# A graph-network step on one core: a dense half in loops of four groups with its input loaded twice, and index copies one group ahead of the indirect transfers

## The reference

```python
h = relu(layernorm(x)); x = x + L0(h)   # three mean-aggregating dense layers
h = relu(layernorm(x)); x = x + L1(h)   # mean of (h[src]-e) by dst and of (h[dst]-e) by src, three products, batch norm
h = relu(layernorm(x)); x = x + L2(h)   # message sum by dst, then a GRU cell on every node
h = relu(layernorm(x)); x = x + L3(h)   # mean by src of h[dst] @ W.T + b
```

## Time and profile before

| | us |
|---|---|
| median of 3 runs | 7257.24 |
| lowest and highest | 7256.88 and 7260.77 |
| the profiled execution | 7259.3 |
| its span | 7257.6 |
| PE busy in the span | 4886.5 (67%) |
| DVE busy | 3986.4 (55%) |
| ACT busy | 2906.5 (40%) |
| POOL busy | 4063.4 (56%) |

### The profile page before, as it was taken

One profiled execution on the slowest core, in us unless ns is written; L12 is line 12 of the kernel. 1 busy time (PEld: TensorE's weight loads), 2 busy tenths in 40 slices (PEclk: granted clock), 3 DMA queues, 4 the chain that ended last, 5 costly groups with the idle time before them and its releaser, 6 DMA issues. The chain is left out here.

```text
span 7257.6 us, 107414 instructions
## 1 busy us (share of the span) xinstructions
PE 4886.5 (67%) x23937; PEld 3569.4 (49%) x23937; DVE 3986.4 (55%) x14866; ACT 2906.5 (40%) x6394; POOL 4063.4 (56%) x4659
## 2 busy tenths in 40 slices
PE   4776735558687687733655636699999978844553
PEld 2454524335565466633553324476666644434553
DVE  5665646654564455743323205566999989843210
ACT  0565634433463364323101100246888855533000
POOL 0655556630550353666565660475888877655556
PEclk9998867779899898865788877557999989955766
DMA  2233346659458655954546537443444444434443
GB/s 84 95 109 101 108 148 192 193 170 326 142 179 273 199 175 186 293 161 135 157 145 140 103 43 227 139 129 133 172 170 171 170 138 146 122 105 123 79 70 47
DMA packets 1124775, 1088.58 MB, mean 150 GB/s; under 512 B 106450, under 2 KB 986241, under 8 KB 1124197
## 3 DMA queue, kind: packets, MB, share of 16 engines
q1 hardware_dynamic: 983746, 911.02, 39.7%
q0 software_dynamic: 140800, 175.08, 11.3%
HBM read 651.65 MB, written 456.06 MB: 153 GB/s over the span
## 5 line engine op out<-in xcount | busy, mean ns | idle before, releaser
L1058 POOL DMA_INDIRECT G_x<-node_table,G_idx x400 | 398.5, 996 | 165.6 <-issue 130.0
L1058 POOL DMA_INDIRECT G_V<-layer_rows,G_idx x400 | 380.6, 952 | 149.0 <-issue 107.3
L1911 PE MATMUL bank<-O_r,O_eq 125*125 125x128 f32 x1600 | 289.6, 365 | 242.2 <-ACT O_out L1937 209.5
L1088 PE MATMUL bank<-first_last_indicators,G_V 125*128 (+1 forms) x1600 | 282.0, 298 | 239.6 <-DVE G_V L1737 151.0
L1070 POOL DMA_INDIRECT out<-O_out,O_idx x200 | 315.8, 1579 | 215.5 <-DMA out<-O_out,O_idx 154.5
L1417 PE MATMUL bank<-B_S,B_V 127*128 127x125 f32 x2000 | 317.8, 302 | 156.8 <-DVE B_S L1405 107.4
L1070 POOL DMA_INDIRECT node_table<-H_out,H_idx x200 | 319.8, 1599 | 169.4 <-DMA node_table<-H_out,H_idx 114.0
L1911 PEld LDWEIGHTS bank<-O_r,O_eq 125*125 125x125 f32 x1600 | 282.2, 278 | 249.6 <-issue 168.8
L1055 POOL COPY G_idx<-i_tb 128x4 int32<-128x4 int32 (+1 forms) x100 | 18.7, 187 | 687.1 <-POOLq L255 523.7
L1088 PEld LDWEIGHTS bank<-first_last_indicators,G_V 125*128 125x128 f32 x1600 | 276.3, 260 | 249.9 <-issue 169.5
L1417 PEld LDWEIGHTS bank<-B_S,B_V 127*128 127x128 f32 x2000 | 276.8, 210 | 192.4 <-issue 122.5
(11 more groups left out here) (472 smaller groups left out, 15868.5 us busy)
## 6 DMA issues: line engine op xcount, KB each, us to landing
P_x<-node_table SPq DMA_DIRECT2D x196, 512.0 KB
B_V<-values SPq DMA_DIRECT2D x250, 256.0 KB
B_krow<-keys_dst SPq DMA_DIRECT2D x250, 250.0 KB
values<-G_V SPq DMA_DIRECT2D x200, 256.0 KB
BN_g<-node_table SPq DMA_DIRECT2D x195, 256.0 KB
out<-P_out SPq DMA_DIRECT2D x195, 256.0 KB
node_table<-G_xg SPq DMA_DIRECT2D x97, 512.0 KB
layer_rows<-A_a SPq DMA_DIRECT2D x100, 256.0 KB
```

Of the source, the lines that this page charges most:

```text
L1058: pool.indirect_dma_start(out=rows[u % len(rows)][:, c, :], out_offset=None, in_=table, in_offset=bass.IndirectOffsetOnAxis(ap=idx[u % len ...
L1088: last = nc.tensor.matmul(m.bank[7][:, bass.ds((i * TILE + c) * 2, 2)], V[0:EP, c, :], m.ind[0:EP, bass.ds(i * TILE + c, 1), :].rearrange( ...
L1911: last = nc.tensor.matmul(m.bank[2 + u % 2][0:EP, d * D:(d + 1) * D], eq[u][:, c, d * EP:(d + 1) * EP], r[u][:, c, :], start=(c == 0), sto ...
```

## The change

Two parts. **In the dense half**, x has 4 buffers instead of 8 and is loaded a second time, into 4 buffers `xr`, one step ahead of the x + C that reads it; `xg` has 4 buffers instead of 8; G, its evacuation and the store come one step earlier (i-4 instead of i-5); one wait of ACT on G is gone; DVE's x + C waits for `xr` and for the store of group i-6 instead of i-10; the loop has 4 steps (groups 8 to 43 are in it). On SP the edge part's store comes first in a step. **In every stage with indirect transfers** POOL copies the indices of group i+1 and then issues the four DMAs of group i. The copy waits for the landing of the transfers that used its `idx` buffer. `take` has 4 buffers instead of 8, and B5's loop on POOL 4 steps instead of 8.

```diff
-        x = [sb(f"x{k}", [128, TILE, D]) for k in range(8)]
+        x = [sb(f"x{k}", [128, TILE, D]) for k in range(4)]
+        xr = [sb(f"xr{k}", [128, TILE, D]) for k in range(4)]
...
-        xg = [sb(f"xg{k}", [128, TILE, 2 * D]) for k in range(8)]
+        xg = [sb(f"xg{k}", [128, TILE, 2 * D]) for k in range(4)]
...
-        FIRST, START, LAST = -5, -2, n + 4
+        FIRST, START, LAST = -4, -2, n + 3
...
-                if has(i + 5):
+                if has(i + 4):
+                    if has(i):
+                        sp.wait_ge(s_n1, i + 1)
+                    sp.dma_start(x[u][:], x_dram[bass.ds(base_of(i + 4), ROWS), :].rearrange("(p j) f -> p j f", j=TILE)).then_inc(s_x[u], 16)
+                if has(i + 1):
+                    v = (u + 1) % 4
                     if has(i - 3):
-                        sp.wait_ge(s_n1, i - 2)
                         sp.wait_ge(s_x1, i - 2)
-                    v = (u + 5) % 8
-                    sp.dma_start(x[v][:], x_dram[bass.ds(base_of(i + 5), ROWS), :].rearrange("(p j) f -> p j f", j=TILE))\
-                      .then_inc(s_x[v], 16)
-                if has(i - 5):
-                    sp.wait_ge(s_g, i - 4)
-                    sp.wait_ge(s_x1, i - 4)
+                    sp.dma_start(xr[v][:], x_dram[bass.ds(base_of(i + 1), ROWS), :].rearrange("(p j) f -> p j f", j=TILE)).then_inc(s_xr[v], 16)
+                if has(i - 4):
+                    sp.wait_ge(s_g, i - 3)
+                    sp.wait_ge(s_x1, i - 3)
...
                 if has(i - 2):
-                    v = (u - 2) % 8
+                    v = (u - 2) % 4
                     dve.wait_ge(s_C, i - 1)
-                    if has(i - 10):
-                        dve.wait_ge(s_st[v], slot_value(i - 10, v, 8))
-                    nc.vector.tensor_tensor(xg[v][:, :, 0:D], pC[:].rearrange("p (j f) -> p j f", j=TILE), x[v][:], ALU.add)\
+                    dve.wait_ge(s_xr[v], slot_value(i - 2, v))
+                    if has(i - 6):
+                        dve.wait_ge(s_st[v], slot_value(i - 6, v))
+                    nc.vector.tensor_tensor(xg[v][:, :, 0:D], pC[:].rearrange("p (j f) -> p j f", j=TILE), xr[v][:], ALU.add)\
...
                 if has(i - 4):
-                    if has(i - 6):
-                        act.wait_ge(s_G, i - 5)
                     evac(hT[p][:], pT2[:], ACT.Copy, s_T2, i - 4, s_h)
...
-        together(eng, ([own(eng)] if own else []) + ([other(eng)] if other else []), unroll=8, back=10, ahead=5)
+        together(eng, ([other(eng)] if other and first_other else []) + ([own(eng)] if own else []) + ([other(eng)] if other and not first_other else []),
+                 back=7, ahead=4)
...
+def next_index(nc, f, index, idx, s_idx, g, w, landed=None):
+
+    if f.has(g):
+        if landed:
+            f.landed(landed, g - 4, w % 4, 64)
+        nc.gpsimd.tensor_copy(idx[w % 4][:], index[:, bass.ds(g * TILE, TILE)]).then_inc(s_idx, 1)
...
-        idx = P.slots("idx", [128, TILE], I32, count=8)
-        V_whole, V = gathered(P, "V", count=8)
...
-                f.landed(s_vo, i - 8, u)
-                f.after(s_hl, i - 8)
-                gather(nc, pool, f, m.i_tb, idx, s_i, i, u, table, V_whole, s_g)
-
-            return 0, n, n - 1, 0, body
+                next_index(nc, f, m.i_tb, idx, s_i, i + 1, u + 1, s_g)
+                if has(i):
+                    f.landed(s_vo, i - 4, u)
+                    f.after(s_hl, i - 4)
+                    gather(nc, pool, f, idx, s_i, i, u, table, V_whole, s_g)
+
+            return -1, n, n - 1, 0, body
```

More of the change, by code:

```diff
@@ L1218, in body @@
                     f = Flow(pool, has, m)
-                    f.after(s_h, i - 4)
-                    f.landed(s_xo, i - 4, u)
-                    gather(nc, pool, f, m.i_src, idx_s, s_is, i, u, a["x"], xs_whole, s_gs)
-                    gather(nc, pool, f, m.i_dst, idx_d, s_id, i, u, a["x"], xd_whole, s_gd)
-                sweep(pool, 0, n, n - 1, body, back=4, ahead=0, special=0)
+                    next_index(nc, f, m.i_src, idx_s, s_is, i + 1, u + 1, s_gs)
+                    next_index(nc, f, m.i_dst, idx_d, s_id, i + 1, u + 1, s_gd)
+                    if has(i):
+                        f.after(s_h, i - 4)
+                        f.landed(s_xo, i - 4, u)
+                        gather(nc, pool, f, idx_s, s_is, i, u, a["x"], xs_whole, s_gs)
+                        gather(nc, pool, f, idx_d, s_id, i, u, a["x"], xd_whole, s_gd)
+                sweep(pool, -1, n, n - 1, body, back=4, ahead=1, special=0)
             @block.sync
@@ L1697, in body @@
                     f = Flow(pool, has, m)
-                    f.after(s_h, i - 4)
-                    gather(nc, pool, f, m.i_src2, idx, s_i, i, u, m.XH, x_whole, s_g)
-                sweep(pool, 0, n, n - 1, body, back=4, ahead=0, special=0)
+                    next_index(nc, f, m.i_src2, idx, s_i, i + 1, u + 1, s_g)
+                    if has(i):
+                        f.after(s_h, i - 4)
+                        gather(nc, pool, f, idx, s_i, i, u, m.XH, x_whole, s_g)
+                sweep(pool, -1, n, n - 1, body, back=4, ahead=1, special=0)
             @block.sync
@@ L1791, in body @@
                     f = Flow(pool, has, m)
-                    f.after(s_g, i)
-                    f.landed(s_sc, i - 4, u, 64)
-                    scatter(nc, pool, f, m.i_dst2f1, idx, s_i, i, u, m.XH, g_whole, s_sc)
-                sweep(pool, 0, n, n - 1, body, back=4, ahead=0, special=0)
+                    next_index(nc, f, m.i_dst2f1, idx, s_i, i + 1, u + 1, s_sc)
+                    if has(i):
+                        f.after(s_g, i)
+                        scatter(nc, pool, f, idx, s_i, i, u, m.XH, g_whole, s_sc)
+                sweep(pool, -1, n, n - 1, body, back=4, ahead=1, special=0)
                 finish(pool, s_sc, n, 64)
@@ L1945, in body @@
                     f = Flow(pool, has, m)
-                    f.after(s_o, i)
-                    f.landed(s_sc, i - 4, u, 64)
-                    scatter(nc, pool, f, index, idx, s_i, i, u, table, out_whole, s_sc, add=True)
-                sweep(pool, 0, n, n - 1, body, back=4, ahead=0, special=0)
+                    next_index(nc, f, index, idx, s_i, i + 1, u + 1, s_sc)
+                    if has(i):
+                        f.after(s_o, i)
+                        scatter(nc, pool, f, idx, s_i, i, u, table, out_whole, s_sc, add=True)
+                sweep(pool, -1, n, n - 1, body, back=4, ahead=1, special=0)
                 finish(pool, s_sc, n, 64)
@@ L2053, in body @@
                     f = Flow(pool, has, m)
-                    f.after(s_x2, i - 4)
-                    gather(nc, pool, f, m.i_src, idx, s_i, i, u, m.XG, x_whole, s_g)
-                sweep(pool, 0, n, n - 1, body, back=4, ahead=0, special=0)
+                    next_index(nc, f, m.i_src, idx, s_i, i + 1, u + 1, s_g)
+                    if has(i):
+                        f.after(s_x2, i - 4)
+                        gather(nc, pool, f, idx, s_i, i, u, m.XG, x_whole, s_g)
+                sweep(pool, -1, n, n - 1, body, back=4, ahead=1, special=0)
             @block.sync
@@ L2560, in body @@
                     f = Flow(pool, has, m)
-                    f.landed(s_x, i, u)
-                    scatter(nc, pool, f, m.i_dstf, idx, s_i, i, u, m.out, x_whole, s_sc)
-                sweep(pool, 0, n, n - 1, body, back=4, ahead=0, special=0)
+                    next_index(nc, f, m.i_dstf, idx, s_i, i + 1, u + 1, s_sc)
+                    if has(i):
+                        f.landed(s_x, i, u)
+                        scatter(nc, pool, f, idx, s_i, i, u, m.out, x_whole, s_sc)
+                sweep(pool, -1, n, n - 1, body, back=4, ahead=1, special=0)
                 finish(pool, s_sc, n, 64)
```

94 lines of the change are left out of this document (49 added, 45 removed).

## The result

The changed kernel took 7522.16 us (median of 4 runs, 7519.24 to 7527.24) against 7257.06 for the kernel before on the same chip: a ratio of 1.0365, 95% interval 1.0347 to 1.0383. It is 265 us slower where I forecast 56 us faster, and outside my range.

A forecast was written before the change was run, and what follows sets the result against it. POOL was taken to pace scatter and gather stages and its transfers to slow the dense half. O1 15, B4 10, B3 5, G1 and G2 22, chunk ends 4: 56 us less, 7203 against 7259.3; range 7125 to 7340.

The forecast's parts named there:

- the term for positions and lookup: Dense chunk beside POOL's 200 transfers in each stage: 0 change; in positions from 10 gained to 63 lost.
- A's term: Stage A, two gathers to a group: 0 change, at most 54 us gained or 8 lost.
- O1's: Stage O1, index copy ahead shortens POOL's step: 15 us gained, 31 at most, nothing at least.
- My slower rival: Uninterrupted POOL starves the dense half, mainly positions and lookup: 63 us more, 7320 us; chance 0.30.
- the 30 us of O1, B4 and B3: Gains of 15, 10 and 5 us from the copy ahead, which the slower rival kept.
- G3's start: Written-out groups with copy gap 0.27 but pace 5.89 us: the gap doesn't set G3's pace, 0 gained.
- The POOL step: O1's step of four DMAs, four gaps of 0.30 and a copy: 5.29 us instead of 5.93.
- H and O2: Transfers there wait for the previous group's landing and the copy lies inside that wait: 0 gained.
- Four buffers in `take`: G1 and G2: opening cut from 36 transfers to 20, 11 us gained in each, between 0 and 21.
- B5: Stage B5, DVE busy 422 of 481 us, so POOL's gaps cost nothing: 0 gained.
- x read twice and the second wait of x + C: Dense half: x's extra traffic and later load covered, 0, at most 10 us lost over the four chunks.
- the first rival: Every POOL gap comes back in the gather and scatter stages: 190 us less, 7067 us; chance 0.10.

The follow-up runs named there:

- prompt chip: Chip kind where no "remote" wait appears from 200 us on, whatever the kernel; the kernel before takes 6849 and 6848 us there.
- take4: The kernel before with four buffers instead of eight in `take`, nothing else, on a prompt chip: 6852.66 us, ratio 1.0008.
- take4_third: The kernel before with four buffers instead of eight in `take`, on the chip where before takes 7388.62 us: 7356.43 us, ratio 0.9957.
- o1_wide: The kernel before with O1's index copy one group ahead and 128 times as wide, on a prompt chip: 6830.04 us, ratio 0.9977.
- wait_back: The changed kernel, with POOL waiting for the copy of group i+1 before issuing group i's transfers: 7263.64 us, ratio 1.0011.
- ahead_only: The kernel before with index copies one group ahead in every stage, old dense half, eight buffers in `take`: 7640.4 us, ratio 1.0533.
- pause_mid: dense_only plus B5's copy ahead and four-step POOL loop, and a waited memset after two of four transfers in positions, lookup, `take`; prompt chip: 6935.16 us.
- dense_only: The kernel before with the changed dense half and four buffers in `take`, index copies in their old place: 7196.61 us, ratio 0.9914.
- sets 2 and 4: Follow-up runs on prompt chips, where the kernel before takes 6849 and 6848 us; the changed kernel ran in the latter: 6561.9 us.
- sets 1 and 3: Follow-up runs on chips where the kernel before takes 7258 and 7246 us; the changed kernel repeated in the latter: 7510.95 us.
- set 4: Follow-up runs on a prompt chip, including the changed kernel: 6561.9 us against 6848.36 for the kernel before, ratio 0.9579.
- set 5: Follow-up runs, including take4_third, on a chip where the kernel before takes 7388.62 us.

## Why the prediction was wrong, step by step

- **The step that failed** is the term for positions and lookup: "by 0.59 us for each transfer the total of 200 stays what it is". I had the dense pace with and without POOL's transfers, and divided. The loss isn't a price of a transfer: it depends on the pauses between them. With the wait put back, positions takes 361.0 us instead of 470.0. Beside the same 200 transfers the chunk ran at 5.83 us a group on a prompt chip instead of 7.44 (4.50 is its free pace in the earlier trace rows), and without pauses at 23.5 on this one. Positions, lookup: forecast 0, measured +119 and +24. The same premise, that closing POOL's gap costs the others nothing, stood under A's term (0, at most 8 lost: measured 125 lost) and O1's (15 gained: 60 lost).
- **My slower rival had the mechanism**, with chance 0.30, but sized it at 7320. It assumed that progress falls in proportion with the pause and took the pause as halved, 14.5 us a group; from 1.2 to 0.5 it would be 0.42 and 18 us, and it was 23.5. Lookup it had about right (30, measured 24). But it kept the 30 us of O1, B4 and B3 as gains, said nothing of A, and let G1 and G2 lose their gain, which they kept. I had thought of starving as a matter of the dense half. But stages in which POOL's transfers need other engines' work a few groups later have it as well: A +125, O1 +60, B3 +30, B4 +13, G3 +9. (G4 with P3 is +12, within the 15 by which it differs between traces of the same code.)
- **G3's start was misread.** In the earlier trace rows the written-out groups had the short gap of 0.27 and the same pace as the loop. I concluded that the gap doesn't set the pace. The better reading, which A's start shares, was that the short gap costs elsewhere what it saves: A's start had runs of 40 and 32 transfers with stops of 7.6 and 7.8 us behind them. The same code on a prompt chip bears this out: in take4's trace A has no stop above 1.7 us, and G3's first 36 transfers run at 5.49 us a group instead of 5.9, without the stop of 5.2 us that before has behind 36. The control for this change stood in the trace of before, and so did ACT's 35 us in the earlier trace rows.
- **The POOL step itself was right**: forecast 5.29, measured 5.19; H and O2 unchanged, as said (-1.7 and -4.5). On a prompt chip O1 gained 36 and B4 36, a little above the 31 that were my most.
- **Four buffers in `take`**: opening of about 20 transfers forecast; in after POOL stops behind 16, 18 stand in the first 27 us, and ACT's wait for its first input is 11.9 us in all, where the earlier trace rows had 35.0. That part is right in mechanism; of its size take4_third shows only that it lies within my 0 to 21 each. On a prompt chip, where ACT has no such wait even with eight buffers (o1_wide), it is nothing. Some 30 us more in each of G1 and G2 come from the dense half's change, which I put at 4 in all.

```profile
2077.00:2104.00 27.00, 17.03 (x18) 0.63 0.58 178
```

```profile
ACT G_h0T L444 <- DMA A_x_dst<-x,A_idx_d: 11.9, 2, 7.7
```

- **B5**: forecast 0 since DVE bounds it; measured -35.5, and 37 on a prompt chip. That reading was wrong: in its loop POOL, with four transfers, two operations of its own, a copy and the gap, set the pace. It waits for hardly anything but its own copy, and its step falls from 8.9 us to 8.0 with the gap (in ahead_only and pause_mid, with the same code in B5, for a part of the loop only: 468.8 and 464.1 us). The loop of four steps isn't the cause: wait_back has it too, and with the wait B5 takes 489.9 us. The rows are of wait_back and of after:

```profile
6138.05 0.19 POOL L1064 COPY B_idx<-i_dst 128x4 int32 x1
6139.06 1.03 POOL L1071 DMA_INDIRECT B_x<-node_table,B_idx  x1 [0.82 <-POOL B_idx L1064]
```

```profile
6335.60 0.18 POOL L1064 COPY B_idx<-i_dst 128x4 int32 x1
6335.95 1.03 POOL L1071 DMA_INDIRECT B_x<-node_table,B_idx  x1 [0.18 <-issue]
```

- x read twice and the second wait of x + C: 0 to 10 forecast, some 10 in positions and lookup each by dense_only, 2 to 7 on a prompt chip. Small, and on the bad side of my range.

What the chip does in those 0.3 us gaps, and why the chips of sets 2 and 4 don't do it, no run here shows. What is shown is the pair: transfers without a longer gap, and updates that arrive late, where the result and sets 1 and 3 were measured, and neither late updates nor a loss with the changed kernel on set 4's chip. On the chips of sets 2 and 5 the changed kernel didn't run; on set 2's no update comes late, and on set 5's they do, where before is slowest. That it is a semaphore update that comes late is read from the profile's "remote"; it was not measured by itself.

The rule of the Trainium skill that I had set beside the first rival, "Perfetto Trace Analysis", Optimization Strategy (close the gaps of the most occupied engine), gives the prompt chip's result and the opposite of the others'. Its reading of consistent bubbles, in the same section, as a sign of missing buffers doesn't fit POOL's gap of 0.88 us: that one was the wait for its own copy, and on the slower kind of chip the other engines depended on it.

## What to carry to other kernels

A gap that repeats on an engine that issues transfers may be what lets the other engines keep up. Before closing it, look for a stretch of the same trace in which it is already short, and at what the others do there: idle time without a named releaser, and a stop of the issuing engine behind each run, are the signs. And where a result hangs on such timing, measure it on more than one chip: here one kernel was 3.65% slower and 4.2% faster.

## What the runs showed of the hardware that I had not expected

- While POOL issues indirect transfers with 0.30 us between them and no longer pause, the other engines' updates came late in the result and in sets 1 and 3 (one wait of DVE in positions lasted 37.1 us), and not on set 4's chip, with the same code.
- 0.88 us of idle after every four transfers kept the loss small (O1 293 us); 0.65 us of POOL's own work in that place nearly so (301); 0.20 us of it did not (352). In A, one pause for eight transfers was not enough, one for four was.
- The kernel before itself takes 6849 us on the one kind of chip and 7246 to 7389 on the other. By take4's trace beside before's, nearly all of the 408 us lies in positions, lookup, A, G1 and G2; from B4 on the stages agree within 15 us.
- In B5, where POOL works 2.3 us on operations of its own between its groups of four transfers, cutting the gap behind the copy from 0.82 to 0.18 us gained up to 35 us on the slower kind of chip and 37 on the other.
